# Relaying freed and filled ring slots in fewer instructions: a two-graph-layer kernel on one Trainium2 core

## What is computed

```python
h = jnp.maximum(_layernorm(x, axis=-1), 0.0)
x = x + _L0_gnn_ref(h, src, dst, ...)      # GAT: softmax over each node's incoming edges
h = jnp.maximum(_layernorm(x, axis=-1), 0.0)
x = x + _L1_gnn_ref(h, edge_index, ...)    # two GCN layers, each:
    h = x @ W
    msgs = h[src] * norm[:, None]
    agg = jax.ops.segment_sum(msgs, dst, num_segments=n_nodes)
    agg = agg + h * (SELF_LOOP_W * dinv * dinv)[:, None]
```

## Time and profile before

| | us |
|---|---|
| median of 3 runs | 5374.18 (5372.75 to 5381.17) |
| the profiled execution | 5383.65 |
| its span, first to last instruction | 5381.5 |
| of it, GAT aggregation (1107 to 2422) | 1315 |
| of it, first GCN aggregation (2637 to 3865) | 1228 |
| of it, second GCN aggregation (4110 to 5332) | 1222 |

### The profile page before, as it was taken

How to read it: one execution, slowest core, us unless ns; L and a number is a source line. 1 busy time by engine, 2 the same in 40 slices (tenths; PEclk the granted TensorE clock), 3 DMA queues, 4 the chain that set the end, 5 groups by cost and what they waited for, 6 DMA issues and landing times.

```text
span 5381.5 us, 82588 instructions
## 1 busy us (share of the span) xinstructions
PE 3719.0 (69%) x15674; PEld 2068.6 (38%) x15675; DVE 2792.5 (52%) x4907; ACT 2086.3 (39%) x5120; POOL 2651.4 (49%) x2782
## 2 busy tenths in 40 slices
PE   4430399866676777779767676777797766777764
PEld 3210398345555555654322222222343222222221
DVE  6300298855665666677444444444553444444445
ACT  3100165134444444445334343434443343444444
POOL 2667300055555555543365565656403666565653
PEclk8765699988988888989888888889898888888987
DMA  7610022365555555555555555555514555555557
GB/s 241 139 46 5 20 60 77 128 185 160 167 160 155 156 153 148 160 147 184 171 172 164 162 172 165 168 156 168 149 68 156 168 170 166 162 166 164 172 163 240
DMA packets 327907, 798.07 MB, mean 148 GB/s; under 512 B 85656, under 2 KB 107818, under 8 KB 326921
## 3 DMA queue, kind: packets, MB, share of 16 engines
q0 software_dynamic: 201376, 631.37, 40.7%
q1 hardware_dynamic: 109241, 134.08, 7.8%
q10 hardware_dynamic: 17232, 31.99, 2.0%
HBM read 712.03 MB, written 84.78 MB: 148 GB/s over the span
## 4 chain that ended last, share of the span: by engine, by line
PE 46%; issue 25%; DVE 8%; another core or an unknown queue 7%; DVEq 4%; SPq 4%; ACT 3%; DMA 2%; ACTq 0%; POOL 0%; POOLq 0%
PE mm L1648 13%; PE tr L1648 10%; PE mm L1477 5%; DVE big L862 3%; PE mm L1626 3%; PE mm L1570 3%; PE sm L1626 3%; SPq L1079 3%; PE tr L1570 3%; PE sm L1514 2%; DVE edge L836 2%; PE tr L1626 1%; PE hist_ps L1626 1%; ACT eler_hots L1397 1%
## 5 line engine op out<-in xcount | busy, mean ns | idle before, releaser
L1274 POOL DMA_INDIRECT edge<-h_tab,row_idx x1564 | 1481.9, 948 | 1223.0 <-SPq L1085 543.9
L1648 PE MATMUL mm<-edge,eler_hots 128*128 x1664 | 945.1, 691 | 571.0 <-issue 320.9
L1397 ACT ACTIVATE eler_hots<-eler_hots,ones 128x256 f32<-128x256 f32 x1272 | 639.2, 502 | 1389.4 <-PE mm L1648 521.8
L1648 PE MATMUL tr<-edge,eler_hots 128*128 x1664 | 900.0, 666 | 172.5 <-issue 102.1
L1274 POOL DMA_INDIRECT rows_wmat<-v_tab,row_idx x782 | 740.8, 947 | 558.6 <-SPq L1085 347.5
L862 DVE TENSOR_TENSOR big<-big,mm 128x512 f32 x832 | 571.8, 687 | 724.3 <-PE mm L1648 439.0
L1388 ACT ACTIVATE eler_hots<-iota,ndrel 128x128 f32<-128x128 f32 x2544 | 882.0, 393 | 157.5 <-issue 0.7
L862 DVE TENSOR_TENSOR big<-big,tr 128x512 f32 x832 | 571.8, 687 | 643.7 <-PE tr L1648 255.4
L1648 PEld LDWEIGHTS mm<-edge,eler_hots 128*128 128x128 f32 x1664 | 326.3, 212 | 1140.8 <-issue 1139.9
L1648 PEld LDWEIGHTS tr<-edge,eler_hots 128*128 128x128 f32 x1664 | 347.6, 215 | 690.4 <-issue 689.1
L1626 PE MATMUL mm<-edge,eler_hots 128*128 128x260 f32 x1176 | 419.0, 442 | 257.5 <-ACT eler_hots L1397 154.5
(11 more groups left out here) (242 smaller groups left out, 3531.7 us busy)
## 6 DMA issues: line engine op xcount, KB each, us to landing
h_tab<-rows_wmat SPq DMA_DIRECT2D x98, 256.0 KB, 2.0
edge<-h_tab,row_idx POOLq DMA_INDIRECT x1564
rows_wmat<-low_tab SPq DMA_DIRECT2D x133, 128.0 KB
ht_tab<-rows_wmat SPq DMA_DIRECT2D x49, 256.0 KB
big<-ht_tab ACTq DMA_DIRECT2D x49, 256.0 KB
v_tab<-rows_wmat ACTq DMA_DIRECT2D x49, 256.0 KB
x_tab<-big SPq DMA_DIRECT2D x49, 256.0 KB, 3.0
rows_wmat<-v_tab,row_idx POOLq DMA_INDIRECT x782
```

The source lines that it names most:

```text
L1274: pool.indirect_dma_start(ring[:, 2 * u + i, :], None, tab, bass.IndirectOffsetOnAxis(ap=row_idx[:, b, n:n + 1], axis=0)).then_inc(a["rows ...
L1397: act.activation(onehot[:, s.j % 2, :, :], dist[:, :, :], ACT.Relu, bias=ones[:, 0:1], scale=-1.0).then_inc(a["onehot_set"], 1)
L1648: pe.matmul(sum_ps[bank][:, :], onehot[:, s.j // 2 % 2, s.j % 2, :], edge[:, ds(slot[0][s.j], D)], start=True, stop=True).then_inc(a["step ...
```

## The change

SP's relay works on **tokens** instead of units. `PER` says how many units a token has: one in the GAT aggregation, two in the GCN ones. A loop turn is one pass around the ring (6 tokens of one unit, or 4 tokens of two); a nested loop of two passes alternates the halves of `row_idx`. Once per pass, at its first token, SP issues one `load_idx` for the next pass (12 columns in the GAT, 16 in the GCN aggregations) and reads the ends of all tokens of the pass; the lag is one token everywhere. POOL waits once per token, and for row numbers once per pass. PE of a GCN aggregation waits for `rows_ready` every four steps, at two numbers per 8 steps, and for `acc_added` every two steps (at a count that covers both banks); DVE waits for `step_sum` every two steps (until both sums are there).

```diff
-IDX = 24
-PER_IDX = IDX // 2
-GPAD = -(-J // IDX) * IDX
+PER = {2: 1, 1: 2}
+IDX = {c: 2 * RING[c] for c in RING}
+GPAD = -(-J // IDX[2]) * IDX[2]
+NEED = 4
@@ DVE, aggregate
-                        dve.wait_ge(a["step_sum"], w + 1)
+                        if s.j % 2 == 0:
+                            dve.wait_ge(a["step_sum"], w + 2)
@@ SP, relay
-                units, freed, free = a["units"], a["freed"], [None]
-
-                def step(s):
-                    g, u = s.k, s.j % units
-                    sp.wait_ge(a["rows_in"][u], s.turn * (2 * PER_IDX // units * 32) + (s.j // units * 32 + 32 + a["rows_before"][u]))
-                    sp.sem_inc(a["rows_ready"], 1)
-                    if s.j % PER_IDX == 0 and (s.inner or g + PER_IDX < UNITS):
-                        load_idx((s.turn * 2 + (s.j // PER_IDX + 1)) * IDX, (s.j // PER_IDX + 1) % 2)
-                    if s.j % 4 == 0:
...
-                    if s.past(freed):
-                        sp.wait_ge(done, free[0][s.j % 4])
-                        sp.sem_inc(a["slot_free"], 1)
...
-                pipelined(sp, UNITS, 2 * PER_IDX, 0, step)
+                units, per, count = a["units"], a["per"], a["count"]
+                turns = -(-count // units)
+
+                def round_of(turn, idx_at, inner):
+                    tokens = units if inner else min(units, count - turn * units)
+                    free = []
+                    for u in range(tokens):
+                        g = turn * units + u
+                        here = per if inner else min(per, UNITS - g * per)
+                        sp.wait_ge(a["rows_in"][u], turn * (32 * per) + (32 * here + a["rows_before"][u]))
+                        sp.sem_inc(a["rows_ready"], here)
+                        if u == 0:
+                            if inner or turn + 1 < turns:
+                                load_idx(a, turn + 1, idx_at)
+                            skip = 0 if inner or turn else 1
+                            _, ends = nc.values_load_multi_w_load_instructions(
+                                ends_row[:, ds(g + skip - 1, tokens - skip)], engines=(mybir.EngineType.SP,), min_val=1,
+                                max_val=a["cut"].steps)
+                            free = [None] * skip + list(ends)
+                        if inner or g >= 1:
+                            sp.wait_ge(done, free[u])
+                            sp.sem_inc(a["slot_free"], 1)
...
+                pairs = (count // units - 2) // 2
+                round_of(0, a["idx"], False)
+                with sp.Fori(0, pairs) as i:
+                    with sp.Fori(0, 2) as half:
+                        round_of(i * 2 + (half + 1), half * a["idx"], True)
@@ POOL, gather
-                    g, u, b = s.k, s.j % a["units"], s.j // PER_IDX
-                    if s.past(a["units"]):
-                        wait_alone("pool", pool, a["slot_free"], g - a["units"] + 1)
-                    if s.j % PER_IDX == 0:
-                        wait_alone("pool", pool, idx_in[b], s.turn * 16 + (16 + a["idx_before"][b]))
+                    g, u, b = s.k, s.j % units, s.j // units
+                    here = per if s.inner else min(per, UNITS - g * per)
+                    if s.past(units):
+                        wait_alone("pool", pool, a["slot_free"], g - units + 1)
+                    if u == 0:
+                        wait_alone("pool", pool, idx_in, s.turn * 32 + (16 * b + 16 + a["idx_before"]))
...
-                pipelined(pool, UNITS, 2 * PER_IDX, 0, step)
+                pipelined(pool, a["count"], 2 * units, 0, step)
@@ PE, aggregate
-                            need_row[1][:, ds(s.turn * (OFFS // 2), OFFS // 2)], engines=(mybir.EngineType.PE,),
+                            need_row[1][:, ds(s.turn * (OFFS // NEED), OFFS // NEED)], engines=(mybir.EngineType.PE,),
+                    if s.j % NEED == 0:
+                        pe.wait_ge(a["rows_ready"], need[0][s.j // NEED])
                     if s.j % 2 == 0:
                         pe.wait_ge(a["onehot_set"], s.turn * (OFFS // 2) + (s.j // 2 + 1))
-                        pe.wait_ge(a["rows_ready"], need[0][s.j // 2])
-                    if s.past(BANKS):
-                        pe.wait_ge(a["acc_added"], w - BANKS + 1)
+                        if s.past(BANKS):
+                            pe.wait_ge(a["acc_added"], w - BANKS + 2)
```

74 lines of the change are left out of this document (41 added, 33 removed).

## The result

The kernel after takes 5418.0 us (median of 20 runs) where the kernel before takes 5380.2 us (20 runs): a ratio of 1.0066, with an interval of 1.0048 to 1.0084. It is slower, where I had forecast 5294 us. In two later batches of runs (e9 to e16) five executions took 4957 to 9942 us at a granted clock of 0.56 to 0.66, where the others took about 4145; medians and ratios there go by the others.

What follows compares the result with a forecast made beforehand. POOL's gather pace (978 us per GCN aggregation) plus 280 us blocked, nearly all on SP's `slot_free`, amid dear sequencer instructions, was taken as the bound. GCN -45 and -45, GAT +10 made -80: 5374 to 5294 us, range 5165 to 5430.

Steps and rivals of the forecast that it cites:

- The GAT term: GAT aggregation: SP's changed relay loop, with 15% more instructions, was forecast to cost 10 us, between -5 and +30.
- the sign named in the prediction: GAT aggregation: a POOL group waiting for SP's copy would show row numbers landing late, at up to 65 us.
- My 0 for them: Copies of row numbers, more frequent and issued one token ahead, were taken as hidden: 0 us, 65 kept for the range.
- The GCN gain: GCN aggregations: fewer sequencer instructions on PE, DVE and SP were to save 45 us per layer, 90 for both.
- what I called decoding there: DVE's add in fast GCN passages: a dropped wait and its decoding, some 0.07 us, 7 us per layer.
- Half is given back by longer runs: GCN aggregations: of 75 us by PE's count only 38 were taken, as longer POOL runs make instructions dear.
- Waiting for the pair: GCN aggregations: DVE and PE starting only in pairs was costed at 0; with no cover, 391 us for 416 pairs.
- Dear instructions come with POOL's unbroken run: GCN aggregations: sequencer instructions get ten times dearer some ten us into an unbroken run of gathers.
- Rival 1: GCN aggregations: coupling by tokens makes PE wait for SP's `rows_ready`, 137 us more over both layers, 5431 us; chance 0.25.
- Rival 2: GCN aggregations: slow passages mostly go, 112 us saved per layer, 5150 us in all; chance 0.14.
- Rival 3: Whole kernel: no change, 5374 us within 0.2%, as POOL's runs alone set the loss or shorter loops free nothing; chance 0.13.

Runs made afterwards that it cites:

- e9: Kernel before with PE's rarer GCN waits, and SP reading unit ends two at a time instead of four in all aggregations: ratio 1.0002, kernel before at 4143 us.
- e16: Kernel after with its relay's inner loop of two passes written out as one loop: ratio 1.0020, where the kernel before takes 4148 us.
- e1: Kernel after, but SP's relay and POOL's gather of the GAT aggregation as before: ratio 0.9924, GAT 1306 us.
- e7: Kernel after, but SP reads the GAT ends three at a time, twice a pass, instead of six at once: ratio 1.0001, GAT 1351 us.
- e10: Kernel before, but SP reads the GAT ends six at once instead of four: ratio 1.0019, GAT 989 us, kernel before at 4143 us.
- e13: The kernel of e9 again in another batch: ratio 1.0007, where the kernel before takes 4148 us.
- e14: The kernel of e10 again in another batch: ratio 1.0027, GAT 989 us, where the kernel before takes 4148 us.
- e17: Kernel before with GAT ends read six at once and GAT row numbers copied in two halves: ratio 1.0020, GAT 987 us, kernel before at 4144 us.
- e2: Kernel before with only PE's and DVE's GCN waits made rarer, SP and POOL as before: ratio 0.9875, GCN 1197 and 1198 us.
- e5: Kernel before with only PE's GCN waits made rarer: ratio 0.9863, GCN 1193 and 1194 us.
- e4: Kernel before with a small memset and a wait on POOL ahead of each GCN gather, gathers 1.90 us apart: ratio 1.0972.
- e3: Kernel before, but GCN gathers fetch rows of 1 KB instead of 2 KB, so sums differ: ratio 1.0010.
- e8: The kernel of e2 with a short POOL pause ahead of every fourth GCN gather: ratio 0.9842, GCN 1191 and 1190 us.
- e15: Kernel before, with GAT row numbers copied in two halves of 12 columns, one every six units: ratio 0.9996, kernel before at 4148 us.

## Why the prediction was wrong

**The GAT term** is the step that failed: +10 us on record, +89 measured, with -5 to +30 in the forecast and bounds that reached to 206. The count was right (SP's 1897 sequencer instructions in that stage became 2180, 15% more, as forecast). But I priced it by the count, through DVE's wait for `rows_ready`, and that wait even fell, from 86.1 us to 53.7 (`rows_ready` line, who waited for it, GAT aggregation of the kernel after):

```profile
  DVE edge L839: 53.7, 39
```

What grew was POOL's wait for `slot_free`, 347.5 us to 456.7. "Mostly because DVE is not done" was the right reading of it, before and after (138 and then 229 us of it until DVE's product, 78 and 80 from there to the grant). What I had wrong is the step behind it: I took DVE's own pace as untouched by an edit of SP's loop, and put the waits of DVE and ACT for PE's signals at nothing. DVE's add waited 215.5 us for such signals before and 318.6 after, and PE, DVE and ACT stood together for 151 and then 249 us. SP's dear instructions in this stage fell meanwhile, from 278 to about 115, and it got slower all the same.

That the relay (with its gathers) brings this is shown by e1. How it does stays open: a clump of three instead of six gives back some 42 of the 89 us (e7), of which the shorter way to the grant is only a part, and what of the loop ends, the double loop and the copies makes the other 47 was tested only where nothing is dear. For the copies the sign named in the prediction is absent: POOL has no wait for one in the GAT aggregation of the kernel after. My 0 for them rested on no row for a copy of that size. The traces of the batches at 5379 to 5413 us time none; those of e10, e13 and e14 put 3.5 us (median) between issue and landing of 12 KB, and that of e17 3.4 us for 6 and for 12 KB. Of its copies of 256 KB those into `h_tab` take 2.0 us, those into `x_tab` 2.9 and those from `x_tab` into `edge` 4.3, so these small copies land no sooner than two of the three large kinds:

```profile
row_idx<-src_group SPq DMA_DIRECT2D x66, 6.0 KB, 3.4
row_idx<-src_group SPq DMA_DIRECT2D x66, 12.0 KB, 3.4
```

**The GCN gain** was 22 and 20 us, for 45 forecast, in the forecast's own lower range. Its parts came out otherwise: PE's part gives 50 and 43 us (38 forecast), DVE's none (7; what I called decoding there is in the chain of the kernel before a piece of 0.05 us named "issue" between two of DVE's, and what it is no row tells), and SP's shorter relay, of which I had counted 34% fewer instructions in its favour, takes 11 to 24 us back. So the count was a price on one engine only, PE. "Half is given back by longer runs" is borne out in kind: POOL's runs (no gap over 0.6 us) grew from 6.7 to 8.5 gathers. That the sum of the layers still lies at the forecast's lower end is in part luck: one part was larger than forecast, one nothing, one of the other sign.

**Waiting for the pair** at 0 holds: e2 (1197, 1198) has it on both engines, e5 (1193, 1194) on PE alone.

**Dear instructions come with POOL's unbroken run:** borne out in part. They need POOL's pace (e4) and not the bytes (e3), but a break every fourth gather leaves most of SP's (e8), and the run alone doesn't make them (e9 to e17). What I missed in the trace of before is the second half, the waits that end late; its groups carried "remote", and its chain 7%.

**The rivals.** Rival 1 named the right side with the wrong place: its sign, PE waiting over 100 us per layer for `rows_ready`, is absent (31.6 us in the row above), and the GCN layers are faster. The sign alone wouldn't have decided it: e5 and e2 do show such waits (132.7 and 105.0 us) and are among the fastest. It was the loss in GAT that turned the sum: -42 + 89 + 5 = +52 us, the difference of the spans. Rival 2 would have wanted windows under 1130 us; they came only in the batches at 4140 us, and not by the edit. Rival 3 fails by the 0.66%. In it I read the 18 packets as those of SP's queue; the row names no engine, and the other instruction queue brought 40; that the loop isn't fetched anew is shown by neither.

**Kernels that beat both:** e5, e2 and e8, at 0.984 to 0.988 where the kernel before takes 5380 us, without the token relay, and e1, which has it in the GCN aggregations, at 0.992. e5 with shorter clumps is at 1.000 where the kernel before takes 4140 us.

## What to carry to other kernels

When an engine waits for a relay, cut its wait in two before you blame the relay: until the event that the relay answers, and from there to the signal. Here the first part grew by 91 us and the second by 2, though the relay's line is named for all of it. Fewer dear instructions on the relay (about 115 for 278 in the GAT aggregation) did not help, and a shorter clump of table reads ahead of its signal did, in part. Cut instructions first on the engine whose own sequencer it waits for ("issue" at PE, 173.6 us), since the same cut on DVE, which waited for PE, bought nothing. Where sequencer instructions have maxima of some forty times their median (718 for 17 ns, 820 for 21), look for waits that end late as well (stretches in which several engines stand at once), and time the pair of kernels in more than one batch before believing a per cent.

## What the runs showed of the hardware

- The same program took 5380 us in some batches and 4143 to 4148 us in others. In the first kind sequencer instructions of all four engines take 0.70 us instead of 17 to 150 ns in the later part of an unbroken run of indirect gathers; in the second none does, in runs of 782 gathers (e15, first GCN aggregation: 17 ns is the longest of SP's signals of `rows_ready`, 21 ns of DVE's waits for the last add). The stage before the aggregations, in which POOL gathers too, differs as well: GAT begins at 1106 us in the kernel before and at 721 us in e15; the dense stage behind the GAT aggregation hardly does (236 and 232 us).
- Waits between engines ended five to seven us late in such passages: products over at 1706.34, their semaphore recorded at 1711.75, during the run's last gather; products over at 3253.88, the add begun at 3261.27, after the last gather of the run, which ended at 3259.0. Stretches of over 2.5 us in which PE, DVE and ACT all stand took 151 us of the GAT aggregation before and 249 after, and there are none in e15.
- Gathers 1.90 us apart left 2 dear instructions of 955, gathers of half the bytes 899, a break of 0.65 us every fourth gather 401 (e2, without the break: 462).
- An indirect gather took 0.95 us and, where nothing held it up, started every 1.25 us in both kinds of batch, for half rows (731.71 us for 775) as for whole ones.
- A copy of row numbers landed 3.4 us after its issue at 6 KB and at 12 KB alike (e17; 3.5 us at 12 KB in e10, e13, e14), copies of 256 KB in e17 after 2.0 us (into `h_tab`), 2.9 (into `x_tab`) and 4.3 (from `x_tab` into `edge`).
- A read of the table of ends took SP 1265 ns (median) for six numbers and 666 ns for three (GAT aggregations of the kernel after and of e7).
